# The feed-forward's input side worked out beside the attention, a batch late, and kept as bf16 integers

## What is computed

```python
q = (x @ Wq.T).reshape(B, N, H, d).transpose(0, 2, 1, 3)
kv = (y @ Wkv.T).reshape(B, N2, 2, H, d).transpose(2, 0, 3, 1, 4)
attn = jnp.einsum('bhnd,bhmd->bhnm', q * scale, k)
attn = jnp.where(pad_mask[:, None, :, None], attn, jnp.float32(-1000000000.0))
attn = jax.nn.softmax(attn, axis=-1)
out = jnp.einsum('bhnm,bhmd->bhnd', attn, v)
...
def bitlinear(x, w, b):
    xq = act_quant(rmsnorm(x))
    wq = weight_quant(w)
    return jnp.einsum('bsd,fd->bsf', xq, wq) + b
h = bitlinear(x, w1, b1)
h = jax.nn.gelu(h, approximate=False)
return bitlinear(h, w2, b2)
...
x = x + jnp.tanh(g_xattn[0]) * _L0_xattn_ref(_layernorm(x, axis=-1), ctx_768, mask_BxS_bk0, L0_xattn_Wq, L0_xattn_Wkv)
x = x + jnp.tanh(g_ffn[0]) * _L0_ffn_ref(_layernorm(x, axis=-1), L0_ffn_w1, L0_ffn_b1, L0_ffn_w2, L0_ffn_b2)
```

## Time and profile before

| | us |
|---|---|
| three runs, median (lowest to highest) | 2000.84 (1998.82 to 2001.43) |
| the profiled execution | 2002.04 |
| its span, first to last instruction | 2000.3 |
| DVE's last `divided` of stage A begins at | 1477.5 |
| stage B's first instruction | 1486.9 |

### The profile page before, as it was taken

How to read it: one execution, slowest core, us unless ns; L and a number is a source line. 1 busy time by engine, 2 the same in 40 slices (tenths; PEclk the granted TensorE clock), 3 DMA queues, 4 the chain that set the end, 5 groups by cost and what they waited for, 6 DMA issues and landing times. The chain is left out here.

```text
span 2000.3 us, 39426 instructions
## 1 busy us (share of the span) xinstructions
PE 1886.8 (94%) x13866; PEld 1468.3 (73%) x13923; DVE 1252.8 (63%) x2285; ACT 1069.3 (53%) x1695; POOL 623.3 (31%) x644
## 2 busy tenths in 40 slices
PE   4999999999999999999999999999948999999997
PEld 3888888888888888888888888888834444444443
DVE  3555555554545454555555555555549999999996
ACT  3444444444444443444344444444327999999997
POOL 2101011110101020110101011210018999999994
PEclk9999999999999999999999999999978999999999
DMA  3011211111112111111112111111032222222221
GB/s 116 27 48 59 74 48 43 47 43 47 45 56 80 43 47 43 49 43 47 43 50 72 59 47 43 47 43 43 21 112 76 91 94 94 94 84 89 94 73 38
DMA packets 56104, 120.61 MB, mean 60 GB/s; under 512 B 5597, under 2 KB 5597, under 8 KB 55934
## 3 DMA queue, kind: packets, MB, share of 16 engines
q1 hardware_dynamic: 56062, 120.07, 18.5%
HBM read 101.64 MB, written 29.43 MB: 66 GB/s over the span
## 5 line engine op out<-in xcount | busy, mean ns | idle before, releaser
L412 ACT ACTIVATE prob<-psum,nmax 114x750 f32<-114x750 f32 x256 | 225.4, 885 | 251.5 <-DVE nmax L600 251.5
L338 POOL TENSOR_TENSOR y_l<-y,y_h 128x750 fp32r<-128x750 f32 x96 | 161.8, 1706 | 553.7 <-ACT y_h L398 553.1
L605 DVE TENSOR_TENSOR k_l<-psum,k_h 128x376 fp32r<-128x376 f32 (+1 forms) x256 | 139.7, 546 | 281.3 <-ACT k_h L403 280.9
L403 ACT ACTIVATE k_h<-psum 128x376 fp32r<-128x376 f32 (+1 forms) x256 | 124.0, 484 | 356.0 <-PE psum L839 354.4
L600 DVE TENSOR_REDUCE nmax<-psum 114x1 f32<-114x750 f32 x256 | 228.4, 934 | 103.3 <-PE psum L828 99.1
L839 PE MATMUL psum<-y_h,wkv_h 128*128 128x376 f32 (+1 forms) x768 | 277.2, 361 | 1.1 <-DVE q_l L593 1.1
L839 PE MATMUL psum<-y_h,wkv_l 128*128 128x376 f32 (+1 forms) x768 | 256.1, 333 | 0.0
L839 PE MATMUL psum<-y_l,wkv_h 128*128 128x376 f32 (+1 forms) x768 | 255.9, 333 | 0.0
L849 PE MATMUL psum<-wkv_h,y_h 128*125 128x512 f32 x576 | 237.4, 412 | 0.0
L849 PE MATMUL psum<-wkv_l,y_h 128*125 128x512 f32 x576 | 228.2, 396 | 0.0
L1432 PE MATMUL psum<-w_q,hq_t 128*128 128x512 bf16 x895 | 204.7, 382 | 24.6 <-ACT yo L1288 24.5
(11 more groups left out here) (117 smaller groups left out, 3373.4 us busy)
## 6 DMA issues: line engine op xcount, KB each, us to landing
y<-in_ctx_t SPq DMA_DIRECT2D x32, 1125.0 KB, 8.0
w_part<-in_w_t SPq DMA_DIRECT2D x32, 512.0 KB, 8.2
xb<-in_x SPq DMA_DIRECT2D x56, 256.0 KB, 2.7
ab<-attn_rows SPq DMA_DIRECT2D x56, 256.0 KB, 2.9
out_rows<-yo SPq DMA_DIRECT2D x56, 256.0 KB, 2.0
attn_rows<-vmean_rows SPq DMA_DIRECT2D x32, 336.0 KB
xa<-in_x SPq DMA_DIRECT2D x32, 112.0 KB
attn_rows<-attn SPq DMA_DIRECT2D x32, 112.0 KB
```

The lines of the kernel that those rows point to most:

```text
L338: pool.tensor_tensor(y_l[:, slot, c, :], y[:, c, :], y_h[:, slot, c, :].bitcast(F32), ALU.subtract).then_inc(a_yl, 1)
L403: act.activation(k_h[:, g, s0:s1], ps_proj[k_bank[par][g, hf]][:, 0:s1 - s0], ACT.Copy).then_inc(a_kh, 1)
L412: act.activation(prob[:, e, :], ps_score[e][0:RP], ACT.Exp, bias=nmax[:, i:i + 1], accum_out=den[:, i:i + 1]).then_inc(p.exp, 1)
L605: dve.tensor_tensor(k_l[:, g, s0:s1], ps_proj[k_bank[par][g, hf]][:, 0:s1 - s0], k_h[:, g, s0:s1].bitcast(F32), ALU.subtract).then_inc(a_k ...
```

## The change

Four things are changed together.

- The feed-forward's input side leaves stage B. In period b of stage A (from b = 1) SP loads x and the attention of batch b - 1 as two halves of 112 rows (`ffn_load`), POOL adds them (`ffn_sum`), DVE takes the moments of each half (`ffn_moments`), POOL centres, and adds the gated second bias to x1 (`ffn_centre`), DVE takes the peaks (`ffn_peak`), POOL makes the scales and rounds (`ffn_round`), and SP stores x1b with the clip in one further column (`x1_rows`) and the integers as bf16 (`xq_rows`). In POOL's order the sums and the centring stand ahead of `rstd` and `split_y`, the rounding behind them. In DVE's order the moments stand behind `k_half(0, 1)` and `k_half(1, 0)`, the peaks behind `second_half(2)`. SP no longer fills `attn_rows`, except for the last batch, and its wait for the attention's store moves behind the next context load. The centring adds the negated mean where the old one subtracts the mean.
- The last batch goes through the same helpers in stage B's steps 1 to 5, stored at step 7.
- Stage B loads x1b and xq ready made, in rings of 8 and 4 tiles, and is unrolled by 8 tiles, where it was 4. DVE copies both halves of the turned hidden rows, ACT none. DVE makes the hidden row's scale between the two halves of the hidden copy, ACT has gelu first, then the rounding of s - 1, then squares, then the result. The multiplication with w2 is a step later. The bias row is loaded first; the small scales are made in the middle of stage A.
- At the program's start the mask has 32 partitions, and its flags come back to one partition by a DMA; ACT's queue takes the small loads; the value half of Wkv is loaded and split first; DVE makes the first `y_l`, before `normalise` and the splitting of Wkv, and PE's wait for the whole split becomes two, ahead of their first uses.

The diff, cut to its core:

```diff
...
+        def ffn_sum(pool, h, x1_done):
+            pool.tensor_tensor(f_x[:, h, 0:D], f_c[:, h, :], f_x[:, h, 0:D], ALU.add).then_inc(x1_done, 1)
+        def ffn_moments(dve, h, own, mom_done):
+            dve.bn_stats(f_stats[:, h, :], f_x[:, h, 0:D]).then_inc(own, 1)
+            dve.wait_ge(own, 1)
+            dve.bn_aggr(f_mv[:, h, :], f_stats[:, h, :]).then_inc(mom_done, 1)
+            dve.sem_clear(own)
+        def ffn_centre(pool, h, xc_done, x1b_done, n):
+            c = f_cols[:, h, :]
+            pool.tensor_scalar(c[:, NEGM:NEGM + 1], f_mv[:, h, 0:1], -1.0, 1.0, ALU.mult, ALU.mult).then_inc(own_f, 1)
+            pool.tensor_scalar(c[:, FVAR:FVAR + 1], f_mv[:, h, 1:2], 1.0 + RMS_EPS, LN_EPS * RMS_EPS,
+                               ALU.mult, ALU.add).then_inc(own_f, 1)
+            pool.wait_ge(own_f, 1)
+            pool.tensor_scalar(f_c[:, h, :], f_x[:, h, 0:D], c[:, NEGM:NEGM + 1], 1.0, ALU.add, ALU.mult).then_inc(xc_done, 1)
+            pool.wait_ge(own_f, 2)
+            pool.tensor_tensor(c[:, FAC:FAC + 1], c[:, FVAR:FVAR + 1], half[0:PT, :], ALU.pow).then_inc(own_f, 1)
+            pool.wait_ge(xc_done, n)
+            pool.sem_inc(met_pool, 1)
+            pool.tensor_tensor(f_x[:, h, 0:D], b2_row[:], f_x[:, h, 0:D], ALU.add).then_inc(x1b_done, 1)
+            pool.wait_ge(own_f, 3)
+            pool.sem_clear(own_f)
+        def ffn_peak(dve, h, max_done):
+            dve.tensor_reduce(f_cols[:, h, XMAX:XMAX + 1], f_c[:, h, :], AX.X, ALU.max,
+                              apply_absolute_value=True).then_inc(max_done, 1)
+        def ffn_round(pool, h, out_done):
+            c, clip = f_cols[:, h, :], f_x[:, h, D:D + 1]
+            pool.tensor_scalar(clip, c[:, XMAX:XMAX + 1], c[:, FAC:FAC + 1], CLIP, ALU.mult, ALU.max).then_inc(own_f, 1)
+            pool.wait_ge(own_f, 1)
+            pool.tensor_tensor(c[:, XINV:XINV + 1], clip, minus[0:PT, :], ALU.pow).then_inc(own_f, 1)
+            pool.wait_ge(own_f, 2)
+            pool.tensor_scalar(c[:, XS:XS + 1], c[:, XINV:XINV + 1], LEVELS, c[:, FAC:FAC + 1], ALU.mult, ALU.mult).then_inc(own_f, 1)
+            pool.wait_ge(own_f, 3)
+            pool.tensor_scalar(f_c[:, h, :], f_c[:, h, :], c[:, XS:XS + 1], ROUND, ALU.mult, ALU.add).then_inc(own_f, 1)
+            pool.wait_ge(own_f, 4)
+            pool.tensor_scalar(f_q[:, h, :], f_c[:, h, :], -ROUND, 1.0, ALU.add, ALU.mult).then_inc(out_done, 1)
+            pool.sem_clear(own_f)
...
-                sp.dma_start(mcol8[0:R, :], mask_col).then_inc(a_mask, 16)
-                sp.dma_start(mcol8[RM:RM + R, 0:(B - 1) * NBLK], mask_col[:, NBLK:]).then_inc(a_mask, 16)
+                sp.dma_start(wkv_raw[:, :, D:2 * D], wkv_in[:, :, D:2 * D]).then_inc(a_wv, 16)
+                sp.dma_start(wkv_raw[:, :, 0:D], wkv_in[:, :, 0:D]).then_inc(a_wk, 16)
...
+                    for h in range(2):
+                        sp.wait_ge(f_st[h], 32 * q + ONE)
+                        sp.sem_inc(met_sp, 1)
+                        sp.dma_start(f_x[:, h, 0:D], rows(x_flat, b, 2 * h, 2)).then_inc(f_ld[h], 16)
+                        if h == 0 and whole:
+                            sp.dma_start(f_c[:, 0, :], rows(attn_d, b, 0, 2)).then_inc(f_ld[0], 16)
+                        elif h == 0:
+                            sp.dma_start(f_c[:, 0, :], vmean_d[bass.ds(b, 1), :].to_broadcast([PT, D])).then_inc(f_ld[0], 16)
+                        else:
+                            if whole:
+                                sp.dma_start(f_c[0:R, 1, :], rows(attn_d, b, 2)).then_inc(f_ld[1], 16)
+                            else:
+                                sp.dma_start(f_c[0:R, 1, :], vmean_d[bass.ds(b, 1), :].to_broadcast([R, D])).then_inc(f_ld[1], 16)
+                            sp.dma_start(f_c[R:PT, 1, :], rows(attn_d, b, RB)).then_inc(f_ld[1], 16)
+                def ffn_store(q, b):
+                    for h in range(2):
+                        sp.wait_ge(f_x1b, 2 * q + h + 1)
+                        sp.wait_ge(f_out, 2 * q + h + 1)
+                        sp.sem_inc(met_sp, 1)
+                        sp.dma_start(rows(x1_d, b, 2 * h, 2), f_x[:, h, :]).then_inc(f_st[h], 16)
+                        sp.dma_start(rows(xq_d, b, 2 * h, 2), f_q[:, h, :]).then_inc(f_st[h], 16)
+                def stored(b):
                     sp.wait_ge(last.st, 32 * (b + 1) + ONE)
...
                             ahead(b, j, t)
+                            before = sp.snap(b - 1)
+                            stored(before)
+                            ffn_load(before, before, False)
                             (w1_piece, w2_piece)[i % 2](b, u, j)
+                            ffn_store(before, before)
                             results(b)
                 for b in range(B - 4, B):
...
+                    ffn = not isinstance(b, int) or b >= 1
+                    if ffn:
+                        for h in range(2):
+                            summed(b - 1, h)
+                        for h in range(2):
+                            centred(b - 1, h)
                     if j == 0 and more_pairs(t, 1):
                         rstd(last, t + 1)
                     if loads_ahead(b):
                         split_y(b + 2, j)
-                batches(pool, period, lambda: None)
+                    if ffn:
+                        for h in range(2):
+                            rounded(b - 1, h)
...
+                act.dma_start(mask_bytes, mask_row.rearrange("a (b s) -> (a b) s", s=S)).then_inc(a_mrow, 16)
+                act.wait_ge(a_zero, 2)
+                act.dma_start(xa[0:R, :], rows(x_flat, 0, RB)).then_inc(last.x, 16)
+                act.dma_start(xa[RM:RM + R, :], rows(x_flat, 1, RB)).then_inc(last.x, 16)
+                act.dma_start(mcol8[0:R, :], mask_col).then_inc(a_mask, 16)
+                act.dma_start(mcol8[RM:RM + R, 0:(B - 1) * NBLK], mask_col[:, NBLK:]).then_inc(a_mask, 16)
...
-                dve.wait_ge(a_mask, 48)
-                dve.memset(kind[:], 0).then_inc(a_flag, 1)
-                dve.tensor_reduce(live[:], mask_bytes.rearrange("a (b k r) -> a b k r", k=NBLK, r=R), AX.X, ALU.max).then_inc(a_flag, 1)
...
+                dve.wait_ge(a_mrow, 16)
+                dve.tensor_reduce(live_b[:], mask_bytes.rearrange("b (k r) -> b k r", r=R), AX.X, ALU.max).then_inc(a_flag, 1)
...
+                for c in range(CC):
+                    dve.wait_ge(a_yh, c + 1 + ONE)
+                    dve.tensor_tensor(y_l[:, 0, c, :], y[:, c, :], y_h[:, 0, c, :].bitcast(F32), ALU.subtract).then_inc(a_yl, 1)
...
+                for n, i in enumerate((1, 0)):
+                    w = slice(D * i, D * i + D)
+                    dve.wait_ge(a_whi, n + 1)
+                    dve.tensor_tensor(wkv_l[:, :, w], wkv_raw[:, :, w], wkv_h[:, :, w].bitcast(F32), ALU.subtract).then_inc(a_wlo, 1)
...
                     k_half(m, 0, 0, 1)
+                    if ffn:
+                        x1_moments(b - 1, 0)
                     second_half(last, n1, 1, 0)
                     second_half(last, n1, 1, 1)
                     k_half(m, 0, 1, 0)
+                    if ffn:
+                        x1_moments(b - 1, 1)
                     negated_max(last, n0, 2, 0)
...
                     second_half(last, n1, 2, 1)
+                    if ffn:
+                        for h in range(2):
+                            x1_peak(b - 1, h)
...
                         v_chunk(1, 0, 0)
+                        pe.wait_ge(a_wlo, 2)
                         pe.wait_ge(last.xe, t + 2 + ONE)
...
+                    if exists(k):
+                        if isinstance(k, int) and k >= ENDS:
+                            for h in range(2):
+                                sp.wait_ge(f_last[h], 32)
+                        slot, n = turn(j, u, -2, 4)
+                        if exists(k - 4):
+                            sp.wait_ge(t_xt, k - 4 + 1)
+                            sp.sem_inc(met_sp, 1)
+                        sp.dma_start(xq[:, slot, :], xq_d[bass.ds(k * 128, 128), :]).then_inc(b_xq[slot], 16)
+                        slot, n = turn(j, u, -2, RING)
+                        if exists(k - RING):
+                            sp.wait_ge(t_yo, k - RING + 1)
...
+                    k = s - LAG - 1
+                    if exists(k):
+                        at_, slot = (j - LAG - 1) % 2, (j - LAG - 1) % RING
+                        pool.wait_ge(t_ye, k + 1)
...
+                        pool.tensor_tensor(yo[:, at_, :], yo[:, at_, :], x1[:, slot, 0:D], ALU.add).then_inc(t_yo, 1)
...
+                    if exists(s):
+                        for i in range(2):
+                            seg = hid[:, j % 2, FU * i:FU * i + FU]
+                            act.wait_ge(t_he, 2 * s + i + 1)
+                            act.activation(seg, seg, ACT.Gelu, scale=gelu_in[:, 0:1]).then_inc(t_g, 1)
...
+                                       accum_out=cols[:, j % RING, HSS:HSS + 1]).then_inc(t_ss, 1)
```

(33 more changed lines are left out.)

450 lines of the change are left out of this document (212 added, 238 removed).

## The result

The kernel after takes 2011.14 us (median of 6 runs, 2010.11 to 2013.61), beside 2001.32 for the kernel before (median of 6 runs). The ratio is 1.0049, with a 95% interval of 1.0035 to 1.0063: the change made the kernel slower by half a per cent, where I had forecast 1989 and faster. One of the six runs of before took 6532.87, for a reason that isn't known, and is left out of the ratio.

A forecast was written before the change was run, and what follows sets the result against it. PE was taken to bound stage A, a ring of dependences stage B's step. 2002.0 - 15 (start) + 21.5 (stage A) - 4.5 (seam) - 14.5 (stage B) = 1989.5, given as 1989 us, range 1974 to 2010.

The forecast's parts named there:

- The start, -15: Program start: PE's first product at 12.1 for 28.32, less 1 for a later wait; -15 us, bounds -17 to -10.
- Even periods, +0.6 each: Stage A: second moments ahead of nmax(2) push DVE by 0.7, paid by PE; 15 x 0.6 = 9 us.
- Late odd periods, 7 x 1.5: Stage A: POOL's work slows DVE's three instructions on the weights' piece; 1.5 us a period (0.6 to 5.5), 10.5 in all.
- my first rival: Late odd periods: all three weights instructions slow beside POOL; 38.5 us for 10.5, total 2017; chance 0.14.
- The last period, +2: End of stage A: the last period has no projections to hide the added work behind; +2 us.
- The seam, -4.5: Between stages: only a load ahead of PE's turning, tile 0's squares at 1504.6 for 1509.14; -4.5 us, bounds -2 to -7.
- Stage B, -14.5: Stage B's steps: 8.27 us for 8.57 over 55 steps, 16.5 less, plus 2; -14.5 us, bounds -22 and +2.
- The ring: Stage B's dependences: squares, POOL's root, DVE's scale, hidden copy, gelu, rounding, squares again; 8.2 us a step after the change.
- the last batch's share: Stage B, steps 1 to 5: the last batch's input work on POOL and DVE; +2 us.
- the centring takes 2.0: Rival, stage A: POOL's new centring as slow as the old, not 0.71 us; total about 1998; chance 0.07.
- the step isn't shortened: Rival, stage B: PE or a new wait holds the step at 8.57 us; total 2005.5; chance 0.10.
- The loads behind the context's: Stage A: the moments' loads, issued behind a context load; wait costed at nothing, otherwise PE pays each us beyond 1.5.

The follow-up runs named there:

- e4: Kernel after, all periods: DVE takes the second half's moments right behind the first half's, not ahead of nmax(2); 1974.48 us.
- e12: Kernel after, late odd periods: POOL waits once, ahead of the first y_l, for the end of the second bias sum; 1987.12 us.
- e6: Kernel after, late odd periods: y_l and the second bias sum made by one-input POOL instructions, leaving out the true values; 1969.83 us.
- e7: Kernel before, late odd periods: POOL makes two more subtractions like y_l between the second and third y_l; 2014.94 us.
- e11: Kernel after, late odd periods: POOL's second bias sum stands behind the three y_l, not ahead of them; 1995.82 us.
- e5: Kernel after, late odd periods: ahead of each y_l POOL waits for the end of its own instruction before it; 2004.15 us.
- e2: Kernel after, late odd periods: POOL does a semaphore step and a one-column, one-input instruction ahead of each y_l; 2017.04 us.
- e3: Kernel after, late odd periods: DVE's first weights instruction takes its second number from a column of SBUF; 2014.62 us.
- e10: Kernel after, late odd periods: DVE does a one-column, two-input instruction ahead of the weights' piece; 2015.03 us.
- e8: Kernel after, stage B: PE leaves out 2 of the 16 products with w2 in each step; 2010.75 us.
- e1: Kernel after, late odd periods: DVE's three instructions on the weights' piece moved from behind heads_out(1) to behind k_half(2, 0); 1966.81 us.

## Why the prediction was wrong, step by step

- **The start, -15: -12.9.** The order of work was right in the main, and the times were short. PE's first product with Wkv began at 15.05, not 12.1:

```profile
8.78 0.69 DVE L718 BATCH_NORM_STATS2 x_stats<-xa 114x6 f32<-114x512 f32 x1 [5.66 <-DMA xa<-in_x]
...
9.96 2.63 DVE L808 TENSOR_TENSOR y_l<-y,y_h 128x750 fp32r<-128x750 f32 x3
...
15.05 0.76 PE L1035 MATMUL psum<-wkv_h,y_h 128*125 128x512 f32 x1 [0.72 <-DVE wkv_l L814]
```

  x has landed at 8.78, and DVE takes all three low parts of y behind its moments; I had two of them done by 8.3. Between PE's first product and the first `divided` 0.4 of the gain is lost, where I took 1 off. Inside the bounds (-17 to -10).
- **Even periods, +0.6 each: right** (+0.58 in each of the early and late ones; e4 shows the cause I named). Their sum came out at 5 and not 9, since before had lost 3.1 us to the lower clock in two of them, which after didn't. The stall of 1.67 us that I put into each of the 8 late even periods of before is in 7; the last has none.
- **Late odd periods, 7 x 1.5: the step that failed.** It measured 44.7, 6.4 a period, above even my upper bound of 5.5. The place, the engines and the instructions were right, and they were my first rival too (38.5, with a chance of 0.14). Two things were wrong. First, I worked with a rate (1.98 to 0.55, over the length of the three instructions) where the row of before already shows a hold: L646's 1.17 in the earlier trace rows is 0.62 to the end of POOL's second `y_l` at 840.20, and 0.55. The same sum with POOL's new run, 933.12 - 927.93 + 0.55, is 5.74, to the hundredth what was measured. That agreement is hindsight: there the instruction in hand and the run ended together, so the row doesn't say to which end to count, and to the end of the bias sum in hand (928.71) the sum is 1.33, which is what e12 shows, where POOL idles behind that sum. The row would have given two prices, and I had neither. To have the higher one I would have had to ask how long the run is with no idle time in it: before, the third `y_l` waits 2.28 us for ACT, and after, POOL comes so late that all three are ready. Second, I priced PE's wait by the wait alone and not by the clock behind it, 2.2 of the 6.4. And my reason for the low end, POOL's root beside L648 and L650 in late even periods, was of an instruction on one column that itself was held: it takes 1.50 there for 0.55 in the early periods.

  The Trainium skill (SBUF — State Buffer, "SBUF: two separate sides") says that the port pair which VectorE and GpSimd share is an exclusive lock between a GpSimd instruction and a VectorE one that is in a two-port mode or has two SBUF inputs: whichever begins first has it for its whole instruction, and the other blocks. The trace agrees that it is a hold and no rate, and that GpSimd can be the one that is held. That one-input instructions of GpSimd hold as well (e6) agrees with it too. By that sentence alone the hold would end with the instruction in hand, 0.8 us here, as it did in e6, e7, e11 and e12; in e4 and e5 it went over one boundary, and in after, e2, e3 and e10 over three or more. The measurement decides.
- **The last period, +2: near** (+2.7), but its granted clock fell from 0.94 to 0.83, which was not in the term.
- **The seam, -4.5: -7.5.** What is late next was the bias row, as I said, but it landed 5.0 us behind the stage's beginning and the integers 5.4, where I had 6.3 and 6.8; squares of tile 0 come 15.3 behind the stage's beginning, for the 17.7 of my timeline. A further 0.6 is that the stage begins 8.8 behind the last `divided`, for 9.4.
- **Stage B, -14.5: -23.2.** The ring was read rightly, 8.2 for 8.14; what I added to it wasn't there: 0.07 a step for hops and turns of loops (only one step in eight is longer, by 0.08), and 2 us for the last batch's share, where three steps of 8.42, 8.56 and 8.45 hold 1.1 at most. PE's work, which I put near the step too, does not set it alone: e8.
- **The rivals.** That the centring takes 2.0 is refuted (0.69), that the step isn't shortened too. The loads behind the context's, which I costed at nothing, cost nothing that shows: early odd periods are no longer than before.
- **Direction.** With 44.7 for 10.5 in one step my own sum gives 2024; the seam and stage B, 11.7 better, and the even periods, 4 better, less 2 at the start, bring it near 2011. Of the chance of slower, 0.19, 0.14 hung on that rival, and its point of decision (3.8 us more in a late odd period) was passed in all seven.

## What to carry to other kernels

When work is put on an idle GpSimd, look for the longest stretch in which its instructions will stand back to back, and which VectorE instruction will be asked for inside it. Price that one twice, as waiting for the end of the instruction in hand and as waiting for the rest of the stretch, however small it is: the runs here show both (1.33 and 5.74 us), and the second is the bound to plan by. An instruction that takes longer than elsewhere by just the time to another engine's end is a hold, not a rate; compare the ends before calling a disturbance small. And give TensorE's wait a second term: here a wait of 4.2 us cost 6.4.

## What the hardware showed that I had not expected

- VectorE's SBUF instruction can wait for a whole run of GpSimd's instructions: 5.74 us for 0.75 (after), 6.21 (e2), 5.31 for one column (e10). An idle time lets it in: 0.24 (e5), 0.27 (e12), 0.67 us (e4). A one-input instruction of 0.19 us in the run, with no idle time, does not (e2). In other runs it got in at the first boundary without idle time (e7, e11); what decides is open.
- One-input instructions of GpSimd hold it too, each to its own end: 0.87, 1.20 and 1.06 us are the time to that end and 0.55 (e6).
- Once VectorE has been let in, the two take turns at the ends of instructions, 1.76 to 1.89 us for one of 0.69 (e5, e7, e11, e12).
- A wait of TensorE of 1.7 us in the middle of a period is followed by the lower clock in some late even periods and not in others of the same kernel, at a price of 1.6 us each (before, e1).
